# A macaron block of eight batches on one core: 384- and 128-column score blocks in one bank

## The chip, the core and the metric

The kernel runs as one program on one core of a Trainium2 chip. The metric is device time in microseconds from launch to end. The engines that matter are TensorE (PE in the profile: matmuls, with its weight loads as PEld), VectorE (DVE), ScalarE (ACT), GpSimd (POOL) and SyncE (SP), which issues the transfers. Each engine runs its own list of instructions in order, and the lists meet only at semaphores.

## The reference, cut to what matters

The input is 8 batches of 1024 tokens with 256 features. It passes through six residual layers: a gated feed-forward layer, a chunked linear attention, the feed-forward layer again, a routed low-rank layer, a softmax attention with rotary positions, and the routed layer once more. The change touches the softmax attention alone, which has 16 heads of 16 features:

```python
scores = jnp.einsum('bhqd,bhkd->bhqk', q, k) * scale
causal = jnp.triu(jnp.ones((S, S), dtype=bool), k=1)
scores = jnp.where(causal, -jnp.inf, scores)
attn = jax.nn.softmax(scores, axis=-1)
out = jnp.einsum('bhqk,bhkd->bhqd', attn, v)
```

## The kernel before, in words

Work on a batch has three parts. The **front** computes the first four layers and the rotary q, k and v for two halves of 512 tokens. The **core** is the softmax attention. The **tail** projects its result and runs the last routed layer. Core work on batch b lies beside front work on later batches and tail work on earlier ones.

The order of work is written out by `weave` (line 468), which every engine calls with its own pieces. Time is cut into ticks, 120 to a batch. In a tick an engine does a core step, if the tick has one (`CORE_TICKS`, line 387: four ticks of five), then a piece of each live front and tail. A core step is split into three parts, with front pieces of the two halves between them (parts 0, 1 and 2). On VectorE the core step comes one tick later than on the others (`lag` 1, line 1121). So a core step's place among front pieces is fixed ahead, and what an engine waits for there depends on how far the others have come.

The core works on groups of four heads, four groups to a batch, 32 in all. Each group has two passes over its scores.

The **first pass** finds each row's maximum. `score` (line 743) puts one bank of scores into one of two banks taken in turn by `r_take` (line 449), which waits until VectorE has emptied the bank two uses back. VectorE reduces it at lines 1104 and 1107. A group has 36 such banks, and this pass runs `LEAD` core steps ahead of the second. The maxima go through a transpose and a transfer by SP into two rows of `stq`, so that the second pass subtracts them by its matmul. The transposes of the maxima and of the results (`y_tr_at`) use the same two banks.

The **second pass** has transposed blocks: 128 keys down the partitions, up to 512 queries along the columns. A unit (`tunits`, line 366) is one half c of the queries, one block kb of keys and one pair hp of heads. Blocks below the diagonal have 512 columns. The four blocks that meet the diagonal have 512, 384, 256 and 128. A group has 24 units and each is one core step:

- `tscore(u + 1)` (line 754): for each head j of the pair one matmul into bank j, which waits until ScalarE has read unit u out of that bank.
- ScalarE's exponential (line 1310): two instructions, bank j to `pexp`.
- GpSimd's select (line 1458): zeroes what lies above the diagonal in a unit's first 128 columns, both heads in one instruction, for diagonal units only.
- `values(u - 1)` (line 769), in every second step: for both units of a key block four matmuls with 32 active columns each, one per head, added up in bank 2. At the end of a half ScalarE copies that bank to `ypv` (line 1316).

A step whose number u is even (u from 0 at the first step of the second pass) has `tscore`, one bank of `score`, the front's piece and `values`. An odd one has `tscore`, one bank of `score`, the front's piece and a second bank of `score` (line 396).

## Time and profile before

| | us |
|---|---|
| median of three runs | 2968.49 |
| the three runs | 2968.49, 2950.70, 2970.06 |
| the profiled execution | 2963.63 |
| its span, first to last instruction | 2961.9 |
| PE busy | 2640.6 (89%) |
| DVE busy | 1862.2 (63%) |
| ACT busy | 1230.0 (42%) |
| POOL busy | 754.6 (25%) |
| mean granted TensorE clock | 0.93 of 2.4 GHz |

Busy time is the time that an engine's rows cover. PE rows overlap and their ends are modelled, so a PE that is shown busy may be waiting for a part of it. The profiled execution lies 4.9 us under the median. Between 846 and 2576 us the trace repeats itself from batch to batch, every 348 us or a little less; from 2576 us on there is no front work left, and from 2907 us on no core work.

### The profile page before, as it was taken

How to read it: one execution, taken by the hardware profiler on the slowest of the kernel's cores; microseconds unless marked ns; L12 is line 12 of the kernel's file. 1: busy time of each engine (PE TensorE's matmuls, PEld its weight loads, DVE VectorE, ACT ScalarE, POOL GpSimd, SP SyncE). 2: the span in 40 equal slices, each digit the busy share in tenths (PEclk: the TensorE clock that was granted, in tenths of full speed). 3: DMA queues.
4: the chain of work that ended last, by engine and by line, in shares of the span. 5: the costliest groups of instructions: out<-in, count | busy, mean ns of one | idle time of the engine just before them, and what ended most of it. 6: DMA issues, size and time to landing. Idle time of an engine off the chain costs nothing.

```text
span 2961.9 us, 45503 instructions
## 1 busy us (share of the span) xinstructions
PE 2640.6 (89%) x15278; PEld 1740.0 (59%) x15278; DVE 1862.2 (63%) x5534; ACT 1230.0 (42%) x2802; POOL 754.6 (25%) x1283
## 2 busy tenths in 40 slices
PE   4885899899999999899999999989998999998986
PEld 3563666456655666466665666556664666555644
DVE  5544667666677567666667666675676666766642
ACT  1321244444444444444444444444444444444452
POOL 2321232223222232223322232222322233211111
PEclk8996899989999999999999899999999999999998
DMA  2015103411333113411134113331134121443211
GB/s 59 1 46 134 23 17 80 115 41 25 70 91 98 39 41 82 129 49 45 38 96 123 40 27 68 93 95 45 35 78 123 52 52 23 100 119 76 64 38 47
DMA packets 137423, 193.97 MB, mean 65 GB/s; under 512 B 49439, under 2 KB 111214, under 8 KB 127854
## 3 DMA queue, kind: packets, MB, share of 16 engines
q1 hardware_dynamic: 131808, 190.89, 25.9%
q8 instruction: 129, 2.11, 0.3%
q10 hardware_dynamic: 5390, 0.18, 0.1%
q14 instruction: 96, 0.79, 0.1%
HBM read 122.34 MB, written 67.63 MB: 64 GB/s over the span
## 4 chain that ended last, share of the span: by engine, by line
PE 71%; DVE 16%; DMA 4%; issue 3%; ACT 3%; POOL 2%; SPq 1%; DVEq 0%; ACTq 0%; POOLq 0%
PE bank L765 9%; PE bank L784 9%; PE bank L750 8%; PE bank L587 5%; PE bank L678 4%; PE bank L518 4%; PE bank L567 4%; PE bank L527 3%; PE bank L536 3%; PE bank L692 3%; DVE bank L1104 3%; PE bank L622 2%; PE bank L497 2%; PE bank L633 2%; PE bank L561 2%
## 5 line engine op out<-in xcount | busy, mean ns | idle before, releaser
L1310 ACT ACTIVATE pexp<-bank 128x512 f32<-128x512 f32 (+3 forms) x1536 | 675.8, 497 | 555.1 <-PE bank L765 554.9
L1104 DVE CUSTOM_DVE_ANT_0 bank<-bank,maskneg 128x256 f32<-128x256 f32 (+3 forms) x1024 | 484.9, 511 | 294.1 <-PE bank L750 291.5
L765 PE MATMUL bank<-stq,stk 128*128 128x512 f32 (+3 forms) x1536 | 558.6, 435 | 58.0 <-ACT pexp L1310 54.9
L750 PE MATMUL bank<-stk,stq 128*128 128x512 f32 (+3 forms) x1536 | 512.8, 399 | 100.1 <-DMA stk<-k_halves 31.3
L765 PEld LDWEIGHTS bank<-stq,stk 128*128 128x128 f32 x1536 | 274.5, 200 | 344.3 <-ACT pexp L1310 210.4
L1107 DVE TENSOR_REDUCE mxa<-bank 128x1 f32<-128x512 f32 x512 | 348.7, 685 | 133.2 <-PE bank L750 128.4
L1458 POOL TENSOR_SCALAR_AFFINE_SELECT pexp<-pexp 128x256 f32<-128x256 f32 x512 | 214.3, 425 | 743.0 <-ACT pexp L1310 742.6
L750 PEld LDWEIGHTS bank<-stk,stq 128*128 128x128 f32 x1536 | 288.2, 203 | 184.5 <-issue 120.6
L784 PE MATMUL bank<-pexp,vsm 128*32 128x512 f32 (+3 forms) x3072 | 360.9, 544 | 5.7 <-POOL pexp L1458 5.5
L1376 POOL TENSOR_SCALAR_AFFINE_SELECT arena<-arena 128x512 f32<-128x512 f32 x128 | 78.5, 638 | 416.3 <-ACT arena L1212 416.3
L587 PE MATMUL bank<-arena 32*128 32x256 f32 x1024 | 158.0, 428 | 17.2 <-DVE arena L911 14.2
L1327 POOL TENSOR_SCALAR varep<-mv 128x4 f32<-128x4 f32 x96 | 22.6, 235 | 488.6 <-DVE mv L822 488.6
L1129 ACT COPY xnT<-bank 128x512 f32<-128x512 f32 x160 | 88.8, 602 | 140.3 <-PE bank L497 140.1
L518 PE MATMUL bank<-arena,wk 128*128 128x256 f32 x512 | 141.0, 425 | 6.5 <-DVE arena L852 6.4
L497 PE MATMUL bank<-ident,arena 128*128 128x128 f32 x768 | 119.4, 306 | 30.7 <-DVE arena L828 29.9
L587 PEld LDWEIGHTS bank<-arena 32*128 32x128 f32 x1024 | 95.2, 198 | 69.8 <-issue 51.7
L497 PEld LDWEIGHTS bank<-ident,arena 128*128 128x128 f32 x768 | 101.3, 159 | 54.5 <-DVE arena L828 34.7
L1432 POOL TENSOR_TENSOR arena<-arena 128x1024 f32<-128x1024 f32 x32 | 75.8, 2368 | 224.1 <-DVE arena L1026 224.1
L784 PEld LDWEIGHTS bank<-pexp,vsm 128*32 128x32 f32 x3072 | 63.5, 112 | 117.5 <-issue 89.8
L911 DVE TENSOR_TENSOR arena<-bank,mask 128x512 f32<-128x512 f32 x128 | 82.2, 683 | 77.0 <-PE bank L587 77.0
L518 PEld LDWEIGHTS bank<-arena,wk 128*128 128x128 f32 x512 | 108.3, 217 | 37.5 <-DVE arena L852 10.8
L1150 ACT ACTIVATE arena<-bank 128x512 f32<-128x512 f32 x64 | 38.3, 598 | 207.0 <-PE bank L518 207.0
(186 smaller groups left out, 4204.3 us busy)
## 6 DMA issues: line engine op xcount, KB each, us to landing
stq<-q_halves SPq DMA_DIRECT2D x128, 256.0 KB
arena<-rope_table SPq DMA_DIRECT2D x8, 2048.0 KB
q_halves<-arena SPq DMA_DIRECT2D x32, 512.0 KB, 3.0
k_halves<-arena SPq DMA_DIRECT2D x32, 512.0 KB, 2.8
stk<-k_halves SPq DMA_DIRECT2D x64, 256.0 KB
stk<-k_halves SPq DMA_DIRECT2D x128, 128.0 KB
v_rows<-arena SPq DMA_DIRECT2D x16, 544.0 KB, 4.1
vsm<-v_rows SPq DMA_DIRECT2D x16, 544.0 KB, 3.8
```

What stands on the lines that cost most here:

```text
L497: last = nc.tensor.transpose(bk[:, t * P:(t + 1) * P], src[:, t, k * P:(k + 1) * P], ident[:])
L518: last = mm(bk[:, m * D:(m + 1) * D], wk0[:, k, m * P:(m + 1) * P], xmA[:, h, k], start=k == 0, stop=k == KT - 1)
L567: last = mm(bk, xn[:, k, j * P:(j + 1) * P], wqkv[:, k, D:3 * D], start=k == 0, stop=k == KT - 1)
L587: last = mm(bks[i][:, k * D:(k + 1) * D], khT[rows, k, j * P:(j + 1) * P], qbd[rows, j % 2, k], start=k == 0, stop=k == KT - 1, skip_group ...
L678: mm(bk[:, i * D:(i + 1) * D], xn[:, k, t * P:(t + 1) * P], wf1[:, k], start=k == 0, stop=False)
L750: last = mm(bk[:, col:col + n], stq[b_][:, h % 2, qb * P:(qb + 1) * P], stk[b_][:, h % 2, k0:k0 + n], start=True, stop=True)
L765: mm(ps(j)[:, 0:n], stk[b_][:, j, kb * P:(kb + 1) * P], stq[b_][:, j, (c + 1) * CH - n:(c + 1) * CH], start=True, stop=True).then_inc(s["t ...
L784: last = mm(ps(2)[HP * j:HP * (j + 1), CH - n:CH], vsm[:, kb, at:at + HP], pexp[:, (u - 1 + j // 2) % NPX, j % 2, 0:n], start=kb == 0, sto ...
L1104: last = nc.vector.tensor_tensor_reduce(out=sc, in0=sc, in1=maskneg[:, CH - n:CH], scale=1.0, scalar=LOWEST, op0=ALU.add, op1=ALU.max, acc ...
L1107: last = nc.vector.reduce_max(dst, sc, AX)
L1310: nc.scalar.activation(pexp[:, u % NPX, j, 0:n], ps(j)[:, 0:n], ACT.Exp, scale=DK ** -0.5).then_inc(s["exp_done"], 1)
L1458: nc.gpsimd.affine_select(out=v, in_=v, compare_op=ALU.is_ge, fill=0.0, base=0, pattern=[[0, 2], [1, P]], channel_multiplier=-1).then_inc( ...
```

## The change

Of the four diagonal blocks, those with 384 and 128 columns become one unit of two blocks, side by side in the same bank: blocks 4c+1 and 4c+3 of half c. A group has 20 units in place of 24, so a batch has 80 core steps in place of 96, on two ticks of three in place of four of five. `tscore` issues two matmuls per head for such a unit and signals after the second. One exponential of 512 columns reads both blocks. GpSimd issues one select for each block of a diagonal unit, as many as before. `values` issues eight matmuls for the merged unit, where there were two groups of four. No matmul is taken away or added. The number of ticks to a batch, the front and the tail stay as they were. The 36 banks of the first pass are spread over 20 steps in place of 24, and the constants that place loads, transposes and copies are rewritten for the new numbering, so that each falls on about the same tick.

```diff
-        tunits = [(c, kb, hp) for c in range(NC) for kb in range(4 * (c + 1)) for hp in range(2)]
+        tblocks = [(c, ((kb, CH, 0),)) for c in range(NC) for kb in range(4 * c + 1)]
+        for c in (1, 0):
+            at = [v[0] for v in tblocks].index(c) + 4 * c + 1
+            tblocks[at:at] = [(c, ((4 * c + 1, 3 * P, 0), (4 * c + 3, P, 3 * P))), (c, ((4 * c + 2, 2 * P, 0),))]
+        tunits = [(c, blocks, hp) for c, blocks in tblocks for hp in range(2)]
...
-        LEAD = 30
+        LEAD = 25
...
-        SX = 129
+        SX = 107
...
-            if (4 * tick) // 5 != (4 * (tick - 1)) // 5:
-                CORE_TICKS[tick] = (4 * tick) // 5
+            if (2 * tick) // 3 != (2 * (tick - 1)) // 3:
+                CORE_TICKS[tick] = (2 * tick) // 3
...
-            score_at[SX - LEAD + n // 3 * 2 + (n % 3 + 1) // 2, n % 3 // 2] = divmod(n, NSU)
+            step = n * NTU // NSU
+            score_at[SX - LEAD + step, 1 if n and (n - 1) * NTU // NSU == step else 0] = divmod(n, NSU)
...
-                        mm(ps(j)[:, 0:n], stk[b_][:, j, kb * P:(kb + 1) * P],
-                                  stq[b_][:, j, (c + 1) * CH - n:(c + 1) * CH], start=True, stop=True).then_inc(
-                                      s["t_ps"], 1)
+                        for kb, n, col in blocks:
+                            last = mm(ps(j)[:, col:col + n], stk[b_][:, j, kb * P:(kb + 1) * P],
+                                      stq[b_][:, j, (c + 1) * CH - n:(c + 1) * CH], start=True, stop=True)
+                        last.then_inc(s["t_ps"], 1)
...
-                    for j in range(G):
-                        at = VP * (G * (g % NG) + j)
-                        last = mm(ps(2)[HP * j:HP * (j + 1), CH - n:CH], vsm[:, kb, at:at + HP], pexp[:, (u - 1 + j // 2) % NPX, j % 2, 0:n],
-                                  start=kb == 0, stop=kb == 4 * c + 3, tile_position=(0, HP * j))
+                    for kb, n, col in blocks:
+                        for j in range(G):
+                            at = VP * (G * (g % NG) + j)
+                            last = mm(ps(2)[HP * j:HP * (j + 1), CH - n:CH], vsm[:, kb, at:at + HP],
+                                      pexp[:, (u - 1 + j // 2) % NPX, j % 2, col:col + n], start=kb == 0, stop=kb == 4 * c + 2,
+                                      tile_position=(0, HP * j))
...
-                        v = pexp[:, u % NPX, :, 0:P]
-                        nc.gpsimd.affine_select(out=v, in_=v, compare_op=ALU.is_ge, fill=0.0, base=0, pattern=[[0, 2], [1, P]],
-                                                channel_multiplier=-1).then_inc(s["causal"], 1)
+                        for _, _, col in tunits[u % NTU][1]:
+                            v = pexp[:, u % NPX, :, col:col + P]
+                            last = nc.gpsimd.affine_select(out=v, in_=v, compare_op=ALU.is_ge, fill=0.0, base=0, pattern=[[0, 2], [1, P]],
+                                                           channel_multiplier=-1)
+                        last.then_inc(s["causal"], 1)
```

**ScalarE, the last group of the last batch.** Before, the exponentials of both halves:

```order
L1310 ACTIVATE pexp<-bank 128x512 x4
L1310 ACTIVATE pexp<-bank 128x384 x2
L1316 COPY ypv<-bank 128x512
L1310 ACTIVATE pexp<-bank 128x384 x2
L1310 ACTIVATE pexp<-bank 128x256 x4
L1310 ACTIVATE pexp<-bank 128x128 x4
L1310 ACTIVATE pexp<-bank 128x512 x6
L1316 COPY ypv<-bank 128x512
L1310 ACTIVATE pexp<-bank 128x512 x14
L1310 ACTIVATE pexp<-bank 128x384 x4
L1310 ACTIVATE pexp<-bank 128x256 x4
L1310 ACTIVATE pexp<-bank 128x128 x4
```

The same group after the change (line numbers are those of the changed kernel; the first copy is that of the group before, in both):

```order
L1318 ACTIVATE pexp<-bank 128x512 x6
L1324 COPY ypv<-bank 128x512
L1318 ACTIVATE pexp<-bank 128x512 x2
L1318 ACTIVATE pexp<-bank 128x256 x4
L1318 ACTIVATE pexp<-bank 128x512 x6
L1324 COPY ypv<-bank 128x512
L1318 ACTIVATE pexp<-bank 128x512 x18
L1318 ACTIVATE pexp<-bank 128x256 x4
```

The eight instructions of 384 and the eight of 128 columns have become eight of 512: 40 exponentials in place of 48.

**TensorE, a stretch without front work in the second half of a group.** L765 is `tscore`, L750 `score`, L784 `values`. Before:

```order
L765 MATMUL bank<-stq,stk 128x512 x2
L750 MATMUL bank<-stk,stq 128x512
L784 MATMUL bank<-pexp,vsm 32x512 x4
L765 MATMUL bank<-stq,stk 128x384 x2
L750 MATMUL bank<-stk,stq 128x512 x2
L765 MATMUL bank<-stq,stk 128x384 x2
L750 MATMUL bank<-stk,stq 128x128
L750 MATMUL bank<-stk,stq 128x384
L784 MATMUL bank<-pexp,vsm 32x512 x4
```

After (`tscore` is L772, `score` L757, `values` L792):

```order
L772 MATMUL bank<-stq,stk 128x384
L772 MATMUL bank<-stq,stk 128x128
L757 MATMUL bank<-stk,stq 128x128
L757 MATMUL bank<-stk,stq 128x384
L757 MATMUL bank<-stk,stq 128x512
L772 MATMUL bank<-stq,stk 128x384
L772 MATMUL bank<-stq,stk 128x128
L772 MATMUL bank<-stq,stk 128x384
L772 MATMUL bank<-stq,stk 128x128
L757 MATMUL bank<-stk,stq 128x256 x2
L792 MATMUL bank<-pexp,vsm 32x512 x4
L757 MATMUL bank<-stk,stq 128x512
```

The merged step has four `tscore` matmuls, and the step with `values` now has a second bank of `score` behind it, here the row of 512 columns at the end, where before it had one bank.

## Rows read from the trace of the kernel before

**Rows 1.** Page, first part: busy time, share of the span, instructions

```profile
PE 2640.6 (89%) x15278; PEld 1740.0 (59%) x15278; DVE 1862.2 (63%) x5534; ACT 1230.0 (42%) x2802; POOL 754.6 (25%) x1283
```

**Rows 2.** Windows: stretch, length; busy (instructions) per engine; clock, DMA share, GB/s

```profile
1533.00:1881.00 348.00, 325.62 (x1905) 215.28 (x1904) 228.62 (x688) 152.92 (x350) 92.21 (x157) 0.94 0.28 68
```

**Rows 3.** Windows of line 765 alone: length; PE, PEld busy (instructions); clock, DMA

```profile
1533.00:1596.00 63.00, 18.76 (x50) 9.05 (x50) 0.95 0.42 115
```

**Rows 4.** PE's waits over the whole run: us in total, times, longest

```profile
PE bank L765 <- ACT pexp L1310: 54.9, 68, 2.2
PE bank L750 <- DVE mxa L1104: 29.9, 30, 2.3
PE bank L750 <- DVE mxa L1107: 25.7, 29, 2.8
PE bank L750 <- DVE mxb L1104: 11.2, 29, 1.2
PE bank L784 <- POOL pexp L1458: 5.5, 8, 0.7
PE bank L765 <- DMA stq<-mlo: 2.3, 1, 2.3
```

**Rows 5.** Timeline of PE, last group, no `score`: start, length, what

```profile
2881.22 0.48 PE L765 MATMUL bank<-stq,stk 128*128 128x128 f32 x2
...
2883.01 0.73 PE L765 MATMUL bank<-stq,stk 128*128 128x512 f32 x2
...
2885.52 0.96 PE L765 MATMUL bank<-stq,stk 128*128 128x512 f32 x2
...
2895.14 0.73 PE L765 MATMUL bank<-stq,stk 128*128 128x512 f32 x2
2896.38 0.99 PE L765 MATMUL bank<-stq,stk 128*128 128x512 f32 x2 [0.51 <-ACT pexp L1310]
...
2898.30 0.62 PE L765 MATMUL bank<-stq,stk 128*128 128x384 f32 x2
...
2901.14 0.50 PE L765 MATMUL bank<-stq,stk 128*128 128x256 f32 x2
...
2903.43 0.44 PE L765 MATMUL bank<-stq,stk 128*128 128x128 f32 x2
```

**Rows 6.** Timeline of PE, a stretch with `score` and without front work

```profile
1587.53 0.73 PE L765 MATMUL bank<-stq,stk 128*128 128x512 f32 x2
1588.10 0.74 PE L750 MATMUL bank<-stk,stq 128*128 128x512 f32 x3
1588.78 0.99 PE L765 MATMUL bank<-stq,stk 128*128 128x512 f32 x2
...
1590.93 0.73 PE L765 MATMUL bank<-stq,stk 128*128 128x512 f32 x2
```

**Rows 7.** Chain of waits, 2700 to 2740 us: start, length, what

```profile
2705.12 0.29 PE bank L750 x2
...
2711.15 0.24 PE bank L750
2711.39 0.99 PE bank L784 x8
...
2721.87 0.78 PE bank L784 x8
...
2727.96 0.36 PE bank L784 x8
```

**Rows 8.** Timeline of ACT, last group: two exponentials of 512, two of 128

```profile
2893.83 1.08 ACT L1310 ACTIVATE pexp<-bank 128x512 f32<-128x512 f32 x2 [0.17 <-PE bank L765]
...
2903.85 0.45 ACT L1310 ACTIVATE pexp<-bank 128x128 f32<-128x128 f32 x2 [0.66 <-PE bank L765]
```

**Rows 9.** Page, groups: busy and mean ns of one, then idle before

```profile
L1107 DVE TENSOR_REDUCE mxa<-bank 128x1 f32<-128x512 f32 x512 | 348.7, 685 | 133.2 <-PE bank L750 128.4
L1458 POOL TENSOR_SCALAR_AFFINE_SELECT pexp<-pexp 128x256 f32<-128x256 f32 x512 | 214.3, 425 | 743.0 <-ACT pexp L1310 742.6
```

More of the change, by code:

```diff
@@ L364, in macaron @@
         f_free = [s[f"f_free{i}"] for i in range(3)]
-        tunits = [(c, kb, hp) for c in range(NC) for kb in range(4 * (c + 1)) for hp in range(2)]
+        tblocks = [(c, ((kb, CH, 0),)) for c in range(NC) for kb in range(4 * c + 1)]
[3 more added lines that the diff above has]
+        tunits = [(c, blocks, hp) for c, blocks in tblocks for hp in range(2)]
         NTU = len(tunits)
+        N0 = sum(c == 0 for c, _, _ in tunits)
+        NLATE = sum(c == 1 and blocks[0][0] >= 4 for c, blocks, _ in tunits)
         packs = (((0, 0), (2, 0)), ((3, 0),), ((1, 0), (5, CH)), ((4, 0),), ((4, CH), (6, CH)), ((5, 0),), ((6, 0),), ((7, 0),),
@@ L380, in macaron @@
         NU = NTU * NG
-        DIAG = [u for u, (c, kb, hp) in enumerate(tunits) if kb >= 4 * c]
-        LEAD = 30
+        DIAG = [u for u, (c, blocks, hp) in enumerate(tunits) if blocks[0][0] >= 4 * c]
+        LEAD = 25
         FT = 120
         F_AT = [(FT * b + 4, FT * b + 26) for b in range(NB)]
-        SX = 129
+        SX = 107
         S_END = SX + NU * NB + 8
         CORE_TICKS = {}
-        for tick in range(S_END * 5 // 4 + 2):
-            if (4 * tick) // 5 != (4 * (tick - 1)) // 5:
-                CORE_TICKS[tick] = (4 * tick) // 5
+        for tick in range(S_END * 3 // 2 + 2):
+            if (2 * tick) // 3 != (2 * (tick - 1)) // 3:
+                CORE_TICKS[tick] = (2 * tick) // 3
         G_AT = [FT * (b + 3) for b in range(NB - 2)] + [1014, 1134]
@@ L399, in macaron, with width @@
         for g in range(NG * NB):
-            y_tr_at[SX + NTU * g + 11] = (g, 0)
+            y_tr_at[SX + NTU * g + N0 + 3] = (g, 0)
             y_tr_at[SX + NTU * (g + 1) + 3] = (g, 1)
-        sums_at = {SX + NTU * g + (10, NTU + 2)[c]: (g, c) for g in range(NG * NB) for c in range(NC)}
-        def width(c, kb):
-            return CH - max(0, kb - 4 * c) * P
+        sums_at = {SX + NTU * g + (N0, NTU)[c] + 2: (g, c) for g in range(NG * NB) for c in range(NC)}
+        def width(blocks):
+            return sum(n for _, n, _ in blocks)
         def slot(g, hp):
@@ L756, in tscore @@
                     g, i = divmod(u, NTU)
-                    c, kb, hp = tunits[i]
+                    c, blocks, hp = tunits[i]
                     if i == 0:
                         nc.tensor.wait_ge(max_in[g % 2], 64 * (g // 2 + 1))
-                    n = width(c, kb)
                     b_ = slot(g, hp)
@@ L1303, in core_act @@
                         g, i = divmod(u, NTU)
-                        c, kb, hp = tunits[i]
-                        n = width(c, kb)
+                        n = width(tunits[i][1])
                         if u >= NPX:
@@ L1513, in core_sp @@
                     for b in range(NB):
-                        for k, at in enumerate((SX + NU * b - 7, SX + NU * b + 3)):
+                        for k, at in enumerate((SX + NU * b - NLATE + 1, SX + NU * b + 3)):
                             if t == at:
```

8 lines of the change are left out of this document (4 added, 4 removed).

## The prediction, made before the change had run

> **What bounds the kernel now.** Start with the busy times. PE is busy 89% of the span, DVE 63%, ACT 42%, POOL 25% [rows 1]. In one period of the steady part PE is busy 325.6 of 348 us and DVE 228.6 [rows 2]. So an engine that is not PE can set the time only where PE waits for it. The list of PE's waits says how often that is: 54.9 us in 68 waits for the exponentials, 29.9 + 25.7 + 11.2 = 66.8 us in 88 waits of `score` for VectorE's reductions, 5.5 us for GpSimd's selects [rows 4]. These are waits that the profile sees; a shorter one lies hidden in the modelled ends of the matmuls.
>
> Then ask how PE is paced where it has no front work. In the last group there is no `score` either. A pair of steps with 512 columns takes 2898.30 - 2895.14 = 3.16 us, and its first half, without `values`, takes 2896.38 - 2895.14 = 1.24 us, of which PE idles half a microsecond for ScalarE [rows 5]. With `score` beside it and the same lack of front work, the half without `values` takes 1588.78 - 1587.53 = 1.25 us although three more matmuls (two banks) run in it: they are hidden in the wait. The other half takes 1590.93 - 1588.78 = 2.15 us, against 3.16 - 1.24 = 1.92 without its one bank: there a bank costs 0.23 us [rows 6]. So thin stretches go by the exponentials' round trip, and the rest by PE's own work.
>
> How much is thin? One stretch of 63 us has 50 of the period's 192 `tscore` rows, that is 25 of 96 steps at 2.5 us each, where the mean is 348/96 = 3.6 us [rows 3]. With the shorter thin pieces elsewhere I take a third of the steps; a quarter and a half are the ends.
>
> **The change, part by part.** The sum is made against the profiled execution, 2963.6 us, which lies 4.9 us under the median of the runs, 2968.5.
>
> *PE's stream.* Matmuls and columns are the same before and after. Nothing is saved on them by themselves.
>
> *Fewer calls of `values`.* A call of 512, 384 and 128 columns takes 0.99, 0.78 and 0.36 us on the chain [rows 7]: 0.21 us for each 128 columns and 0.15 us per call. Merging turns 0.78 + 0.36 into 0.99 and saves 0.15 us. There are 2 merged key blocks in each of 32 groups: 64 x 0.15 = 9.6 us. This is PE's own time, so it counts in thick stretches too.
>
> *Fewer round trips, in thin stretches.* The pairs of steps from one start of `tscore` to the next take 2.84 us (384), 2.29 (256), 1.79 (128) and 2.51 (the 512 that follows, which has the 128's `values` in it) [rows 5]: together 9.43. After the change they are 3.16 (merged), 2.29 + 0.21 and 2.51 + 0.21, since `values` trails by a pair and each now has 128 columns more: 8.38. So 1.05 us per merge, 2.1 per group, the 0.15 of each call within it.
> Against it stands `score`. A group's 36 banks now go on 20 steps. The ten without `values` have room for two each, and take 18; the ten with `values` get 18 where 12 had 12. Six more banks at 0.23 us are 1.4 us. Net: 0.7 us per group that is thin. The core work after the front's end, from 2576 to 2907 us, is about six groups: at 24 steps of 1.7 us [rows 6] 331 us would hold eight, and the tail's work lies between. Of the 26 groups beside front work a third is 9, and of the five that follow I take the whole: 14 x 0.7 = 10 us. The last group has no `score` and keeps its 2.1 us.
>
> *Thick stretches.* The other 17 groups keep 2 x 0.15 = 0.3 us each, 5 us in all. Every step is also a point at which PE waits for ScalarE to have caught up; 16 fewer in 96 are a sixth of 54.9, or 9 us.
>
> *ScalarE.* Two exponentials take 1.08 us at 512 columns and 0.45 at 128 [rows 8]: 0.21 per 128 columns and 0.24 fixed. 128 merged units save 0.24 us each, 31 us of ScalarE. It is covered by PE, which is twice as busy; where the cover is gone, it is already in the round trips above. I count nothing more.
>
> *GpSimd.* The selects are as many as before, but the merged unit's two follow each other, and `values` waits for the second: 0.425 us more [rows 9]. `values` comes a whole exponential pair (1.08 us) after its unit's, so this hides. Uncovered in all 128 units it would be 54 us; the 5.5 us of waits [rows 4] say that the cover holds. Zero, with 5 as the upper end.
>
> *SyncE and the transfers.* Loads, row transfers and copies keep their ticks within half a tick. The one that gets tighter is the transfer of the maxima: it has 3 steps in place of 4 before the second pass needs it. It waited once, 2.3 us, in the last group [rows 4]. A step of thin work is about 1.7 us [rows 6], so up to 1.7 us in each of the last five groups: 0 to 8 us, I take 2. No queue is moved past another's work.
>
> *VectorE's two banks.* This is the unknown. A bank of `score` waits for the reduction of the one two back. Before, steps of one and of two banks take turns, four of them on successive ticks and then a tick without. After, two steps on successive ticks have two banks each (one step in five has one), and then comes a tick without. A bank in the second of the two waits for a reduction of 0.685 us [rows 9] that VectorE begins one tick late, with the front's work ahead of it. The tick without a step lets VectorE catch up. The trace cannot show the new pattern. Its waits now cost 66.8 us; a third less is -22 and two thirds more +45. I take +10, near the present cost, since the number of banks is the same and the wait falls partly on time in which PE would have waited for ScalarE.
>
> *The sum.* -10 (thin) -2 (last group) -5 (calls) -9 (sync points) +2 (maxima) +10 (banks) = -14 us. 2963.6 - 14 = 2949.6; I forecast **2950**.
>
> *A rule against it.* One bank of two matmuls stands at 0.29 us in the chain and one of a single matmul at 0.24 [rows 7], so a merged bank reaches ScalarE 0.05 us later than one of 512 columns. The Trainium skill (Perfetto Trace Analysis, "Matmuls") wants independent matmul groups to rotate through banks, so that the evacuation of one overlaps the next, and says in the same place that larger matmuls are more efficient; by the first the merge gives overlap away, by the second it gains. At 0.05 us for 256 banks the loss is 13 us at most, a third of that where the pace is thin: 4 us, inside the range.
>
> **The rivals.**
> *The gain is larger (2915).* PE's busy rows hide waits, so the round trip rules more than a third of the steps. For it: half a microsecond of waiting in a step that shows 0.73 us busy of 1.24 [rows 5]. If all 31 groups with neighbours gain 1.05 x 2 - 1.4 = 0.7 us, if waits for ScalarE and VectorE (121.7 us) fall by a sixth, 20 us, and the banks cost nothing: 22 + 2 + 20 = 44 us, so 2920; some 5 us come on top if the granted clock (0.94 in the period, rows 2) gains from fewer gaps: one hundredth of it is worth 348 x 0.01/0.94 = 3.7 us a period at most. The Trainium skill (Perfetto Trace Analysis, "Identifying the Most-Contended Engine") holds that matmul occupancy is a poor measure of TensorE's headroom and that weight-load occupancy is better; that row is 59% here [rows 1], which agrees with hidden waits. Against it: thick stretches have front matmuls in nearly every step.
> *Slower (3001): the two banks.* In 320 of 640 steps, the second of each two, both banks wait for reductions that VectorE starts in that same tick. Waits of this kind last 66.8/88 = 0.76 us on average and up to 2.8 [rows 4]. At 0.075 us more per such step the 24 us of savings are gone; from 0.18 on the time is over 2998; one full wait in every fourth step, 0.19 us, gives 2963.6 - 24 + 61 = 3001. For it: VectorE is two thirds busy and in order, and its core work comes a tick late. Against it: no reductions lie on the tick before the first of the two steps.
> *Nothing moves (2964).* Instructions on PE are as before and its order is fixed by ticks that have not moved; a wait taken out reappears at the next front piece, which waits for VectorE or ScalarE at the same tick.
>
> **How the numbers follow.** Runs of this kernel spread over 19 us, so within 1% (2939 to 2998 about the median) counts as no change. Forecast, net -14 us, own range 2930 to 2968: 0.45, of which 0.13 under 2939. Larger gain: 0.22. Nothing moves: 0.13. Slower: 0.20, of which 0.17 over 2998. Faster 0.13 + 0.22 = 0.35; slower 0.17; the same 0.48. The range goes from 2905, the larger gain with a better clock, to 3005.
>
> **What would show it.** Exponentials 1280, ACT busy about 1200 us; calls of `values` 320; in the last group a merged pair at 3.16 us and 20 steps where 24 were; PE's waits for the exponentials under 50 us. Right if `score`'s waits for VectorE are 60 to 90 us. Wrong if they pass 110 us (the slower rival) or fall under 50 (the larger gain), or if `values` waits for GpSimd over 10 us.

## The result: slower by 21 us, and the profile after

The changed kernel takes 2985.39 us (median of 12 runs, 2969.74 to 3006.44) against 2964.16 for the kernel before (12 runs, 2950.70 to 2970.06). The ratio is 1.0079, 95% interval 1.0056 to 1.0101: slower, by less than 1%. The forecast was 2950, 14 us faster than the profiled execution of the kernel before; the time moved the other way. The profiled execution took 2974.95 us (span 2973.2), 10 us under its median, so its trace shows about half of the loss.

The page's busy times and two steady periods of the changed kernel (windows: length; busy time and instructions of PE, PEld, DVE, ACT, POOL; granted clock, DMA share, GB/s):

```profile
PE 2601.8 (88%) x15278; PEld 1741.7 (59%) x15278; DVE 1874.9 (63%) x5534; ACT 1194.4 (40%) x2546; POOL 749.6 (25%) x1283
```

```profile
1599.00:1947.00 348.00, 317.78 (x1912) 212.99 (x1904) 229.81 (x688) 148.13 (x319) 91.89 (x156) 0.96 0.27 69
1947.00:2295.00 348.00, 317.67 (x1912) 213.25 (x1904) 229.80 (x688) 148.09 (x319) 91.84 (x156) 0.96 0.27 68
```

ACT fell by 36 us, where 31 had been worked out. PE is busy 318 us of a period, against 326 in [rows 2], and the period is 348 us in both. That looks as if PE had saved 8 us, but the two stretches have different clocks, 0.96 and 0.94. The kernel before also has a period at 0.96 (columns as above):

```profile
1191.00:1532.00 341.00, 318.31 (x1906) 210.99 (x1904) 228.08 (x688) 152.74 (x350) 92.12 (x157) 0.96 0.28 70
```

At the same clock PE is busy for the same time, and the changed kernel's period is 7 us longer: 7 us more in which PE stands. PE's waits over the whole run say where (us in total, times, longest; line 757 is `score`, 772 `tscore`, 792 `values`, 594 the scores of the linear attention):

```profile
PE bank L772 <- ACT pexp L1318: 70.0, 71, 2.2
PE bank L757 <- DVE mxa L1113: 33.9, 39, 2.5
...
PE bank L757 <- DVE mxb L1113: 28.5, 27, 1.7
PE bank L757 <- DVE mxa L1116: 23.1, 47, 2.8
...
PE bank L594 <- DVE arena L920: 21.6, 20, 3.1
...
PE bank L757 <- DVE mlo L1090: 5.6, 7, 1.0
...
PE bank L772 <- DMA stq<-mlo: 4.2, 4, 2.0
...
PE bank L792 <- POOL pexp L1467: 3.5, 6, 0.6
```

The waits for exponentials rose from 54.9 to 70.0 us, where I had expected under 50. `score`'s waits for reductions rose from 66.8 to 33.9 + 28.5 + 23.1 = 85.5 [rows 4]; with the 5.6 for the row maxima they are the 91 of the expectations below. Of the waits that the sum had priced, only those for the selects fell, from 5.5 to 3.5.

The last group, with no `score` and no front, went as forecast. PE's timeline there (start, length, what, in brackets the idle time before it):

```profile
2908.84 0.79 PE L772 MATMUL bank<-stq,stk 128*128 128x384 f32 x4
2910.09 0.99 PE L772 MATMUL bank<-stq,stk 128*128 128x384 f32 x4 [0.46 <-ACT pexp L1318]
...
2912.00 0.51 PE L772 MATMUL bank<-stq,stk 128*128 128x256 f32 x2
```

The merged pair takes 2912.00 - 2908.84 = 3.16 us, the figure put down for it. From the last addition that GpSimd does for a front to the end, the kernel before needs 2961.9 - 2625.7 = 336.2 us and the changed one 2973.2 - 2643.5 = 329.7, 6.5 less (sum: 5.6). The first row is of the kernel before, the second of the changed one:

```profile
2625.71 2.37 POOL L1432 TENSOR_TENSOR arena<-arena 128x1024 f32<-128x1024 f32 x1 [8.54 <-DVE arena L1026]
```

```profile
2643.53 2.36 POOL L1440 TENSOR_TENSOR arena<-arena 128x1024 f32<-128x1024 f32 x1 [7.28 <-DVE arena L1035]
```

So where the core runs by itself, merging shows a gain of the size that was worked out, in one profile each. The loss, 18 us by 2643, lies where front and core share the engines. By the last such addition of each batch the changed kernel is behind by 2.7 us at 898 us, 10.9 at 1251 and 18.2 at 1599; after that nothing is added, since the kernel before takes 348 us for its later periods too, at clocks of 0.94 and 0.95.

### The profile page after: what moved, and what is told of

It is laid out like the page before. It is cut to its first block, busy times and chain, and to the rows that moved or that the text cites. A ratio compares the mean times of both kernels' runs of the same rounds, so it can differ in the third digit from the quotient of the medians.

```text
span 2973.2 us, 45061 instructions
## 1 busy us (share of the span) xinstructions
PE 2601.8 (88%) x15278; PEld 1741.7 (59%) x15278; DVE 1874.9 (63%) x5534; ACT 1194.4 (40%) x2546; POOL 749.6 (25%) x1283
## 4 chain that ended last, share of the span: by engine, by line
PE 65%; DVE 15%; issue 3%; DMA 3%; ACT 2%; POOL 2%; SPq 1%; POOLq 0%; DVEq 0%; ACTq 0%
PE bank L757 9%; PE bank L792 8%; PE bank L772 8%; PE bank L594 4%; PE bank L685 4%; PE bank L525 3%; PE bank L534 3%; PE bank L574 3%; PE bank L543 3%; PE bank L504 3%; PE bank L699 2%; DVE mxa L1116 2%; DVE bank L1113 2%; DVE arena L837 2%; DMA arena<-x_rows 2%
## 5 line engine op out<-in xcount | busy, mean ns | idle before, releaser
L1318 ACT ACTIVATE pexp<-bank 128x512 f32<-128x512 f32 (+1 forms) x1280 | 644.9, 562 | 374.6 <-PE bank L772 374.5
L757 PE MATMUL bank<-stk,stq 128*128 128x512 f32 (+3 forms) x1536 | 549.1, 407 | 122.7 <-DVE mxa L1113 33.9
L772 PE MATMUL bank<-stq,stk 128*128 128x512 f32 (+3 forms) x1536 | 499.9, 411 | 74.6 <-ACT pexp L1318 70.0
L757 PEld LDWEIGHTS bank<-stk,stq 128*128 128x128 f32 x1536 | 283.5, 198 | 374.1 <-issue 319.5
L772 PEld LDWEIGHTS bank<-stq,stk 128*128 128x128 f32 x1536 | 280.1, 201 | 227.8 <-ACT pexp L1318 161.8
L792 PE MATMUL bank<-pexp,vsm 128*32 128x512 f32 (+3 forms) x3072 | 341.1, 534 | 7.1 <-POOL pexp L1467 3.5
L594 PE MATMUL bank<-arena 32*128 32x256 f32 x1024 | 148.6, 407 | 29.3 <-DVE arena L920 21.6
L504 PE MATMUL bank<-ident,arena 128*128 128x128 f32 x768 | 116.8, 302 | 34.1 <-DVE arena L837 33.1
L792 PEld LDWEIGHTS bank<-pexp,vsm 128*32 128x32 f32 x3072 | 70.3, 112 | 129.4 <-issue 106.7
L1221 ACT COPY arena<-bank 128x512 f32<-128x512 f32 x128 | 68.8, 589 | 163.2 <-PE bank L594 163.2
```

The source lines that it names most:

```text
L504: last = nc.tensor.transpose(bk[:, t * P:(t + 1) * P], src[:, t, k * P:(k + 1) * P], ident[:])
L594: last = mm(bks[i][:, k * D:(k + 1) * D], khT[rows, k, j * P:(j + 1) * P], qbd[rows, j % 2, k], start=k == 0, stop=k == KT - 1, skip_group ...
L757: last = mm(bk[:, col:col + n], stq[b_][:, h % 2, qb * P:(qb + 1) * P], stk[b_][:, h % 2, k0:k0 + n], start=True, stop=True)
L772: last = mm(ps(j)[:, col:col + n], stk[b_][:, j, kb * P:(kb + 1) * P], stq[b_][:, j, (c + 1) * CH - n:(c + 1) * CH], start=True, stop=True)
L792: last = mm(ps(2)[HP * j:HP * (j + 1), CH - n:CH], vsm[:, kb, at:at + HP], pexp[:, (u - 1 + j // 2) % NPX, j % 2, col:col + n], start=kb = ...
L1318: nc.scalar.activation(pexp[:, u % NPX, j, 0:n], ps(j)[:, 0:n], ACT.Exp, scale=DK ** -0.5).then_inc(s["exp_done"], 1)
```

## The experiments

Times are medians, with the ratio to the kernel before on the same chip and its 95% interval.

**First question: the reductions, or the ticks without a step?** In the two light kernels VectorE reduces only the last 128 columns of each block, so a part of the maximum is left out.

```diff
-                            sc = r_bank("s", g, i)[:, col:col + n]
+                            sc = r_bank("s", g, i)[:, col + n - P:col + n]
```

> The changed kernel with VectorE's reduction of each first-pass score block cut to its last 128 columns (part of the maximum is left out), so that a bank of scores is handed back early. Two theories of the 21 us by which the change is slower (2985 against 2964). Theory 'banks': PE waits on VectorE for the banks of bunched scores (91 us in the changed kernel, 67 before). Then this kernel's waits of the score line on VectorE fall under 35 us and it comes out 5 to 20 us FASTER than the kernel before with the same cut (the next run), since the loss is gone and the fewer core steps remain. Theory 'empty ticks': PE waits longer on ScalarE's exponentials and on the front's chains because the core steps stand in two of three ticks. Then this one stays 12 us or more SLOWER than the kernel before with the same cut, and its waits on exponentials stay at 65 us or more.

> The kernel before with the same cut of VectorE's reduction to 128 columns of each block: the partner of the run above. By both theories its score waits on VectorE fall from 67 us to under 30 and the time falls by 15 to 50 us, to 2915 to 2950; what is compared is this time against the changed kernel's with the same cut: 5 to 20 us above it by 'banks', 12 us or more below it by 'empty ticks'.

Measured: 2913.50 (0.983, 0.9804 to 0.9857) for the changed kernel and 2864.52 (0.9662, 0.9637 to 0.9687) for the one before. The cut gains 72 us in the one and 96 in the other, where 15 to 50 had been expected of e2. `score`'s waits for reductions are 39 and 26 us. Cheaper reductions don't take the loss away: it grows from 21 to 49 us, as "empty ticks" had it, and e1's waits for exponentials are 76.5 us. The length of a reduction, on which my price for the banks rested [rows 9], isn't what the change costs by.

**Second: the placement of the banks alone.** e3 takes the changed kernel and places its 36 banks of a group by ticks, not by core steps; one function more, called by PE and by VectorE in each tick, carries it. e4 does the reverse to the kernel before: two banks in three of four steps.

```diff
-            step = n * NTU // NSU
-            score_at[SX - LEAD + step, 1 if n and (n - 1) * NTU // NSU == step else 0] = divmod(n, NSU)
+            tick = n * 30 // NSU
+            score_at[(SX - LEAD) * 3 // 2 + tick, 1 if n and (n - 1) * 30 // NSU == tick else 0] = divmod(n, NSU)
```

```diff
-            score_at[SX - LEAD + n // 3 * 2 + (n % 3 + 1) // 2, n % 3 // 2] = divmod(n, NSU)
+            score_at[SX - LEAD + n // 2 + n // 6, n % 2] = divmod(n, NSU)
```

> The changed kernel with its full reductions, but the first-pass scores no longer tied to core steps: 36 banks spread evenly over the 30 ticks of a group, ticks without a core step included (six banks in five ticks, against two in nearly every core step and none in every third tick). 'Banks': the score waits on VectorE fall from 91 us to 50 to 70, and the time to 2958 to 2972. 'Empty ticks': what is lost is the wait for exponentials and front chains in the pattern of ticks, which stays: 2978 to 2992; a bank in the tick without a core step gives PE a little work there, so up to 5 us may come back.

> The kernel before with one thing changed, the placement of the first-pass scores: two banks in three of four core steps and none in the fourth, in place of 2, 1 and 1 or so; no tick, unit or exponential moves. 'Banks': score waits on VectorE rise from 67 us to 85 to 100 and the time by 10 to 22 us, to 2974 to 2986. 'Empty ticks': the placement hardly matters: 2960 to 2970.

Measured: e3 2949.35 (0.9955, 0.9937 to 0.9974), e4 3000.55 (1.0130, 1.0103 to 1.0157). The placement alone turns the change from 21 us slower to 11 us faster, and it slows the unchanged units by 40. Neither theory had these two right: e3 is below both ranges and e4 above both. The granted clock doesn't explain the placement's worth. Among the runs with a clock of 0.935, the changed kernel took 2976.01 us, e3 2950.52, e8 (below) 2945.86 to 2950.13 in four, and the kernel before 2954.10 to 2964.02 in three. So about 26 of the 36 us are there at an equal clock; the rest goes with the lower clock of the changed kernel (median of its runs 0.930, of e3's 0.937), and what lowers it isn't shown. These are the waits of e3 (line 761 is `score`, 776 `tscore`):

```profile
PE bank L761 <- DVE mxb L1119: 53.1, 40, 2.2
PE bank L776 <- ACT pexp L1326: 48.1, 66, 2.2
PE bank L761 <- DVE mxa L1119: 46.0, 56, 2.0
...
PE bank L761 <- DVE mxa L1122: 15.7, 24, 2.8
```

The waits for exponentials fell to 48.1, as the forecast had them. `score`'s waits for reductions rose again, to 115 us, in the faster kernel. The list names what PE waits for last at each place; it isn't the price of that place.

**Third: is it cover, and what is the merging worth with banks placed alike?**

```diff
 e5: the placement of e3 with the cut of e1
 e6: the kernel before, with
+            tick = n * 30 // NSU
+            score_at[124 + tick, 1 if n and (n - 1) * 30 // NSU == tick else 0] = divmod(n, NSU)
 e7: the changed kernel, with
+        for step in range(S_END + 1):
+            CORE_TICKS[6 * (step // 4) + step % 4 + 2] = step
 e8: the placement by ticks, with
+        BANK_TICKS = sorted([*range(30), 1, 7, 10, 16, 22, 25])
```

> The changed kernel with the banks spread over all ticks (2949 with full reductions) and VectorE's reduction cut to 128 columns per block as in the two light runs (2914 for the changed kernel, 2865 for the one before). The spreading took 36 us off the changed kernel while PE's score waits on VectorE did not fall (91 before it, 115 and more after). Theory 'ring': the spreading acts on how soon VectorE hands a bank back; with the cut that hardly limits any more, so little is left to gain: 2900 to 2914. Theory 'cover': a bank of scores is PE's own work that stands between a chain's steps (exponential, front reductions); a tick without one leaves the chain bare, and a quicker VectorE doesn't mend that: the spreading gives 30 to 50 us here too, 2862 to 2884, about the kernel before with the same cut.

> The kernel before with the same spreading of the banks over all 30 ticks of a group (its own placement is three banks in two core steps, in four of five ticks, so nearly even). If the merging itself is worth what the sum gave it (about 15 to 20 us from steps, values calls and last groups), this stays near the kernel before, 2950 to 2966, and the merged kernel with the same spreading (2949) is the faster by that. If the merging is worth nothing, this comes to 2940 to 2952 as well.

> The changed kernel with four core steps in a row and then two ticks without, in place of two and one; banks stay tied to steps. 'Cover': two ticks in a row without banks and steps are barer still: 2995 to 3030. 'Ring': second banks of four steps follow one another, so slower as well, 2990 to 3010, with score waits on VectorE over 100 us; what tells them apart is where PE waits: 'cover' has it on exponentials and front lines, their sum up by 20 us or more.

> The changed kernel with one bank in every tick and the six second banks of a group put into ticks without a core step (in the even spreading most of them fall beside a core step). 'Cover': the ticks without a step are the barest, so a little more comes back: 2935 to 2948. 'Ring': two banks in one short tick wait for VectorE: 2950 to 2965.

Measured: e5 2860.78 (0.966, 0.9636 to 0.9684), e6 2980.20 (1.0058, 1.0036 to 1.0080), e7 3017.56 (1.0186, 1.0163 to 1.0210), e8 2947.22 (0.9955, 0.9940 to 0.9969). With the cut, the placement is worth 53 us (2913.50 to 2860.78), more than the 36 without: again not the reductions' length. "Cover" had e7 and e8 in its ranges and missed e5 by 1 us; "ring" had e5, e7 and e8 wrong. In e7 PE waits at the front's lines, whose chains have no core work beside them for two ticks (lines 503 and 524 stand where 504 and 525 do in the changed kernel, which had 33.1 and 8.2 us):

```profile
PE bank L771 <- ACT pexp L1317: 76.6, 66, 3.6
PE bank L503 <- DVE arena L836: 55.1, 21, 6.8
...
PE bank L524 <- DVE arena L860: 25.5, 8, 3.4
```

`score`'s waits for reductions in e8, as fast as e3, are larger still, 138 us:

```profile
PE bank L762 <- DVE mxb L1120: 55.2, 50, 1.9
...
PE bank L762 <- DVE mxa L1120: 46.5, 44, 2.0
PE bank L762 <- DVE mxa L1123: 36.2, 54, 2.8
```

e6 is slower than the kernel before, and above both of its ranges: even spacing isn't good in itself.

**Fourth: a rule for the doubles?** Banks per kind of tick, in the order tick with a step and no `values`, tick without a step, tick with step and `values`: 1, 2, 0.6 (e9), 2, 1, 0.6 (e10), 1, 0.6, 2 (e11), against 1, 1.6, 1 in e8 and 1.8, 0, 1.8 in the changed kernel. e12 is the kernel before with its doubles in ticks without a step.

```diff
 e9
+        BANK_TICKS = sorted([t for t in range(30) if t % 3 < 2] + [t for t in range(30) if t % 3 == 1] + [2, 8, 11, 17, 23, 26])
 e10
+        BANK_TICKS = sorted([t for t in range(30) if t % 3 < 2] + [t for t in range(30) if t % 3 == 0] + [2, 8, 11, 17, 23, 26])
 e11
+        BANK_TICKS = sorted([t for t in range(30) if t % 3 != 1] + [t for t in range(30) if t % 3 == 2] + [1, 7, 10, 16, 22, 25])
 e12
+        BANK_TICKS = sorted([*range(30), 2, 7, 12, 17, 22, 27])
```

> The changed kernel, banks per kind of tick (a tick with a core step but no values call, an empty tick, a tick with a step and a values call): 1, 2, 0.6 in place of the changed kernel's 1.8, 0, 1.8 and the 1, 1.6, 1 of the run before. The steps with a values call last 3.8 us in the changed kernel and the two ticks without one together 5.0, 3.6 and 5.0 where second banks lie in empty ticks. Theory 'even ticks' (PE's own work of a tick must be even, since the chains of the other engines move on one tick at a time): better again, 2930 to 2945. Theory 'ring' (banks must come evenly, whatever lies between): two banks in every empty tick are bunched, 2952 to 2970.

> Banks per kind of tick 2, 1, 0.6: the doubles stand beside the core steps that have no values call. 'Even ticks': the values ticks are as light as in the run before this one, the rest is nearly even: 2932 to 2950. 'Ring': 2952 to 2970, as any two in a tick. If what the second bank harms is the exponential of the same step, by standing between the score block and the values, it is slower than the doubles in empty ticks by 10 us or more.

> The opposite: banks per kind of tick 1, 0.6, 2, the doubles in the ticks that have the values call as well. 'Even ticks': most of the loss is back, 2970 to 2990, though banks are no more bunched than in the two runs before. 'Ring': the same as those two, 2952 to 2970.

> The kernel before with one bank in each tick and the six second ones in its empty ticks (one in five): the placement that gave 2947 with the merged blocks. It tells what the merging is worth with banks placed alike: at 2955 to 2970 the merging is worth 8 to 20 us, as the sum without its term for the banks has it; at 2940 to 2950 the merging is worth nothing and the placement all. 'Even ticks' expects it below the spreading that put all doubles beside values calls (2980), by 10 us or more.

Measured: e9 2959.88 (0.9979, 0.9961 to 0.9997), e10 3000.58 (1.0110, 1.0083 to 1.0136), e11 3002.45 (1.0113, 1.0088 to 1.0138), e12 3025.70 (1.0204, 1.0177 to 1.0231). "Even ticks" falls with e10, and "ring" with the 41 us between e9 and e10, which are bunched alike. e12 is the worst, with the placement that was the best for merged units. "Cover" falls as an account of the time as well: e10 and e12 have a bank in every tick without a step, and are among the slowest. It does describe the waits for exponentials in the merged kernels, 36.7 to 48.6 us with a bank or more in such a tick (e3, e8, e9, e10), 70.0 and 72.5 with none or 0.6 (the changed kernel, e11). So e10's loss, though of the size that was put down for a second bank that harms the exponential, isn't that: its waits for exponentials are 40.3 us, below e8's 48.6. None of the rules put down for kinds of ticks holds.

What goes with the time in most of these kernels is VectorE's idle time just before its two reduction lines, that is, the time in which it stands at a reduction until PE has written the bank (sum of the two groups, one profile each):

| kernel | VectorE idle before reductions, us | median, us |
|---|---|---|
| before | 427.3 | 2964 |
| e8, e14 | 444.4, 453.3 | 2947, 2957 |
| e9, e3 | 453.7, 457.2 | 2960, 2949 |
| e6 | 461.8 | 2980 |
| e10, e12 | 484.4, 490.1 | 3001, 3026 |
| e13, changed | 490.2, 492.3 | 2981, 2985 |
| e11, e4 | 500.2, 500.4 | 3002, 3001 |

This is a sign and not a price. The kernel before has the least and isn't the fastest, and e12 is 25 us slower than e10 with 6 us more. e7, where the core's ticks moved as well, has 446.5 at 3018 and doesn't fit. The light kernels, whose reductions are shorter, have 573 (e2), 622 (e5) and 686 (e1) at 2865, 2861 and 2914. The groups in the changed kernel and in e8 (busy and mean ns of one, then idle time before them):

```profile
L1113 DVE CUSTOM_DVE_ANT_0 bank<-bank,maskneg 128x256 f32<-128x256 f32 (+3 forms) x1024 | 486.7, 510 | 323.6 <-PE bank L757 319.0
...
L1116 DVE TENSOR_REDUCE mxa<-bank 128x1 f32<-128x512 f32 x512 | 349.3, 688 | 168.7 <-PE bank L757 159.6
```

```profile
L1120 DVE CUSTOM_DVE_ANT_0 bank<-bank,maskneg 128x256 f32<-128x256 f32 (+3 forms) x1024 | 483.7, 510 | 243.8 <-PE bank L762 241.9
L1123 DVE TENSOR_REDUCE mxa<-bank 128x1 f32<-128x512 f32 x512 | 349.7, 686 | 200.6 <-PE bank L762 197.1
```

The trace of before showed this column too: 133.2 us of it stand in [rows 9]. I had read it as idle time of an engine that isn't the bottleneck. Since VectorE works in order, it is time in which the front's pieces behind the reduction stand still as well.

**Fifth: one bank, and VectorE's order alone.** A stall of the kind that the slower rival described is in the trace, in the 12th tick of a batch. PE and VectorE there:

```profile
1640.61 0.50 PE L757 MATMUL bank<-stk,stq 128*128 128x512 f32 x1
1640.95 0.69 PE L772 MATMUL bank<-stq,stk 128*128 128x384 f32 x4
1643.92 0.55 PE L757 MATMUL bank<-stk,stq 128*128 128x256 f32 x1 [2.27 <-DVE mxa L1113]
```

```profile
1638.59 1.40 DVE L861 SCALAR_TENSOR_TENSOR arena<-xnT,mu,arena 128x512 f32<-128x512 f32 x2
1639.91 1.37 DVE L837 TENSOR_SCALAR arena<-arena,mv,rstd 128x256 f32<-128x256 f32 x4
1641.20 1.39 DVE L828 BATCH_NORM_STATS2 stats<-arena 128x6 f32<-128x256 f32 x4
1642.63 0.38 DVE L831 BATCH_NORM_AGGREGATE mv<-stats 128x2 f32<-128x6 f32 x4
1642.92 0.27 DVE L1113 CUSTOM_DVE_ANT_0 bank<-bank,maskneg 128x128 f32<-128x128 f32 x1
```

VectorE isn't idle; it has 4.5 us of front pieces ahead of the reduction for which PE stands 2.27 us. The Trainium skill (PSUM — Partial Sum Buffer, "Engine vs sequencer instructions") says that VectorE's queue is strictly first in, first out. These rows agree: the reduction comes behind all the front pieces ahead of it.

e13 moves one of the 144 banks of a batch so that this stall goes; e14 brings it into e8. e15 and e16 leave PE's order alone and shift VectorE's reductions by half a tick; e17 and e18 shift them by less.

```diff
 e13: the changed kernel's placement, written by ticks, and
+            if tick % 120 == 11:
+                tick, part = tick - (part == 0), 0
 e14: e8, for the first group of each batch
+        ONE_MOVED = sorted([*range(30), 1, 8, 10, 16, 22, 25])
 e15: VectorE's two reductions of a tick, in the next tick, each behind one front piece
-                                core(at, 1 + q)
+                                core(at, q if lag else 1 + q)
 e16: e8, the two directly behind the front pieces of their own tick
+                            if first and lag and q < NC:
+                                first(tick, q)
 e17: the changed kernel, at the end of their own tick (e18: the same in e8)
+                            if at is not None and lag and q in (1, 3):
+                                core(at, (1, 3).index(q))
```

> The changed kernel with ONE bank of the 144 of a batch moved: of the two that stand in the 11th tick of each batch, the first goes into the empty 10th. In the changed kernel PE stands 2.3 us at the first bank of the 12th tick, since the two banks of the 11th lie unreduced behind 4.5 us of VectorE's front pieces (normalization and mixing of the next stage); the triple of ticks 12 to 14 takes 16.2 us there and 12.1 with doubles in empty ticks. Theory 'queue' (a bank is held until VectorE has passed the front pieces that stand ahead of its reduction, so it costs only beside such pieces): 3 to 4 us per batch, less what is recovered behind: 2958 to 2972. Theory 'even' (what counts is how evenly the banks of all ticks lie): one of 144 changes nothing, 2980 to 2990.

> The mirror: the version with doubles in empty ticks (2947) with one bank of each batch moved from the empty 10th tick to the 11th, so that two lie ahead of the 12th again. 'Queue': 2958 to 2975. 'Even': 2944 to 2950.

> The changed kernel with VectorE's reductions half a tick later in its own order (each behind one more of VectorE's front pieces); PE's order is as it was, no instruction is added. 'Queue': every bank is held behind one more piece: 3010 to 3080, with the score waits on VectorE well over 120 us. If the place in VectorE's queue doesn't matter: 2980 to 2990.

> The version with doubles in empty ticks (2947), with VectorE's reductions half a tick earlier (a tick's two reductions directly behind that tick's own front pieces). 'Queue': the banks come back earlier: 2925 to 2945, unless VectorE now stands at a reduction for PE and holds its front pieces up, 2950 to 2975; then VectorE's idle time ahead of the reductions rises over the 457 us or so of the changed kernel's.

> The changed kernel with PE's order untouched and VectorE's reductions only a little earlier: the first of a tick ahead of the tail's pieces of the same tick, the second at the end of its tick, ahead of the next tick's first front piece in place of behind it. 'Queue' (a bank costs by what stands ahead of its reduction): the second banks come back one front piece sooner, 2955 to 2978. If VectorE now stands at the reductions for PE as it did with all of them half a tick early (850 us idle ahead of them, 3100), 2990 to 3050. If the order of VectorE's queue isn't what the second banks cost by: 2980 to 2990.

> The same small shift of VectorE's reductions in the version with doubles in empty ticks (2947): second banks are 6 of 36 there, not 16 of 36, so 'queue' has little to give back, 2935 to 2950; if VectorE stands for PE, 2955 to 3000.

| | median, us | ratio, interval | VectorE idle before reductions, us |
|---|---|---|---|
| e13 | 2981.28 | 1.0076, 1.0049 to 1.0103 | 490.2 |
| e14 | 2956.67 | 0.9986, 0.9974 to 0.9998 | 453.3 |
| e15 | 3032.90 | 1.0247, 1.0226 to 1.0268 | 361.3 |
| e16 | 3099.93 | 1.0470, 1.0449 to 1.0490 | 850.0 |
| e17 | 3035.14 | 1.0238, 1.0221 to 1.0256 | 701.8 |
| e18 | 2979.30 | 1.0045, 1.0028 to 1.0062 | 593.9 |

e15 to e18 show that the place of a reduction in VectorE's order sets the time, both ways, with the same work on every engine. Half a tick later PE stands for banks (151 us of `score`'s waits, as expected) and 48 us are lost, although VectorE idles least of all there. Earlier, VectorE stands for PE: 32 us lost in e18, 50 in e17, 153 in e16. (The 457 us in the expectation of e16 are e3's idle time; the changed kernel has 492.3.) In e17 the banks did come back sooner: `score`'s waits for reductions fell from 85.5 to 65.3 us. What VectorE holds up by standing costs more. PE's waits for VectorE in the front, 33.1 + 21.6 + 8.2 = 62.9 us in the changed kernel, are 97.2 in e17:

```profile
PE bank L598 <- DVE arena L924: 41.1, 34, 5.5
PE bank L508 <- DVE arena L841: 37.9, 14, 6.8
...
PE bank L529 <- DVE arena L865: 18.2, 15, 3.4
```

In e18 neither sum moves much from e8's (138 and 52 us, against 138 and 47), so its 32 us don't show in the list. Of the four orders tried on the changed kernel and e8, the one that the program had is the best.

e13 and e14 tell what one such stall is worth. Bringing it in costs 9.5 us (the intervals of e8 and e14 don't overlap): over the seven batches with a front beside them 1.4 us each, where the stall is 2.3. Taking it out gains 4 us that can't be told from nothing. So e13 came where "even" had it and missed "queue", and e14 lies between the two. The stretch of 24 ticks from the stall on shows what comes back (windows of e13, then of the changed kernel, in the same batch: ticks 12 to 14; from there to the 33rd tick; ticks 33 to 35; tick 33 alone; columns as above):

```profile
1633.60:1647.00 13.40, 12.29 (x83) 10.10 (x79) 8.55 (x32) 6.55 (x14) 3.19 (x7) 1.00 0.00 0
1647.00:1706.90 59.90, 54.42 (x256) 34.46 (x253) 39.35 (x133) 25.12 (x61) 13.73 (x22) 0.91 0.17 40
1706.90:1722.40 15.50, 15.50 (x102) 11.74 (x99) 7.43 (x19) 5.53 (x11) 3.45 (x8) 0.78 0.14 37
1706.90:1714.60 7.70, 7.70 (x31) 6.06 (x28) 4.58 (x12) 1.07 (x2) 2.69 (x6) 0.57 0.28 74
```

```profile
1640.90:1657.10 16.20, 13.93 (x80) 11.13 (x79) 8.52 (x33) 6.31 (x13) 3.19 (x7) 0.89 0.01 1
1657.10:1714.00 56.90, 51.07 (x256) 32.30 (x253) 38.53 (x131) 25.00 (x61) 13.09 (x21) 0.98 0.17 43
1714.00:1727.10 13.10, 13.10 (x102) 9.97 (x99) 7.79 (x21) 5.53 (x11) 4.09 (x9) 0.96 0.16 44
1714.00:1719.40 5.40, 5.40 (x32) 4.36 (x29) 4.94 (x14) 1.07 (x2) 2.59 (x6) 0.89 0.39 106
```

Without the stall the first stretch is 2.8 us shorter. Then the same 256 and 102 PE instructions take 75.4 us in place of 70.0, at clocks of 0.91 and 0.78 in place of 0.98 and 0.96. In this batch the saved wait came back, and more, as time at the lower clock. It is the batch with the longest stretch of e13: its 24 ticks take 88.8 us here and 86.5, 83.5, 87.4 and 86.5 in the four others with a full front, against 86.2 to 86.3 in four of the changed kernel's and 91.5 in the fifth. So the return differs from batch to batch. In e14 the three ticks take 16.5 us where e8 has 12.1, in four of the five batches, and there nothing of it comes back within the 24 ticks (88.0 to 88.3 us, against 83.5 to 83.9).

## Why the prediction was wrong

The step that failed is "VectorE's two banks", +10 us: the sum took the new placement of the banks for nearly free, and it costs more than all the other terms gain.

- *Its size.* With the merged units kept and the banks placed otherwise the time is 2949 and 2947, so the placement costs 36 to 38 us (about 26 at an equal clock). The range of that step, -22 to +45, held it; the value I took was the present cost of the waits, not the new pattern's.
- *Its mechanism.* I priced a wait of PE for a reduction of 0.685 us. The cut of the reductions leaves the loss (49 us), and `score`'s waits for reductions are larger in the faster placements (115 us in e3, 55.2 + 46.5 + 36.2 = 138 in e8) than in the changed kernel (85.5). The shifts of VectorE's order show what the sum left out. Two queues, each worked in order, hand each other banks. PE may stand for a bank whose reduction lies behind VectorE's front pieces (e15); VectorE may stand for a bank that PE has not yet written, and then holds up the front pieces that PE needs next (e16, e17). My sum saw the first half alone. The 65.0 us that VectorE stands longer in the trace after (492.3 - 427.3, 59 of it named as waits for `score`) fit the second half. That this half makes the loss of the changed kernel is argued and not shown: no run takes it away by itself.
- *The test I set.* 85.5 us of waits count as "right" (60 to 90) where the time was wrong, and e3 has the 115 of "wrong" and is faster than the kernel before. The test was a poor one.

The other terms:

- *Fewer round trips and calls, -10, -2 and -5: right where they can be seen.* The merged pair takes 3.16 us. The stretch behind the last front is 6.5 us shorter (sum: 5.6, or 3.6 with the maxima's 2). But e13, which differs from the changed kernel by one bank in each batch, needs 336.4 us there, at a clock of 0.89 where the changed kernel has 0.91, so the 6.5 isn't clear of the clock. What the terms are worth beside front work was not measured by itself. Waits for GpSimd fell to 3.5 us, and the maxima's transfer cost 1.9 us more (sum: 2).
- *The front's end.* It is not at 2576 us: the front's last matmuls run to 2624 us and its last addition starts at 2625.7. That leaves 5.6 groups behind it (268 rows of `tscore`, 48 to a group) where I took six, a difference of under half a microsecond in the sum.
- *Sync points, -9: right only where a bank lies between.* The waits for exponentials fell by 6.8 us in e3 and to 48.6 in e8, but rose by 15 us in the changed kernel, whose ticks without a step have no bank either.
- *The rule set against it.* The prediction let larger matmuls speak for the change; but the merge makes no matmul larger, only the exponentials, so nothing was to be had there.
- *Together.* Without the term for the banks the sum was -24. The best placements measured are 11 to 13 us under the kernel before, which would make these terms about half right in front of the whole kernel. But a period of e8 takes 341.2 to 341.7 us in four of five, at clocks of 0.95 to 0.97, and one of the kernel before 341.3 at 0.96, while e8 is 4 to 18 us faster among the whole runs at 0.935. So a part of the 11 to 13 us may come with the clock, and how much isn't shown. With one placement for both, merging is worth 31 us (e6 to e3) or 78 (e12 to e8); how much of that is the merging and how much a placement that suits one of them isn't settled.

Of the rivals, "slower, the two banks" had the sign, its place (the second of two steps) and a wait that the trace shows in the 12th tick, but not the price of it: filling that wait gave nothing that can be measured. Its threshold was a little off too: 0.18 us in 320 steps gives 2997, not over 2998. "The gain is larger" wanted the waits for ScalarE and VectorE to fall by a sixth, and both rose. "A wait taken out reappears" held in some batches of e13, in the one shown through the clock rather than the next front piece.

What stays open: which pairs of ticks make the 36 us. By the mean start times of the ticks over four batches, the largest loss to e8 is 4.1 us in ticks 12 to 14 for the changed kernel, 3.5 in ticks 54 to 56 for e10, and 3.8 in ticks 21 to 23 for e11; e10 loses 2.8 in ticks 21 to 23 too, and e11 3.6 in ticks 12 to 14. These are few places, and the largest is another one each time. No rule that I tried foretold e10 or e12.

The version with doubles in ticks without a step (e8, 2947.22 us, 0.9955, 0.9940 to 0.9969) is, with e3, the fastest with whole reductions: 13 us under the kernel before on its chip, and 38 under the changed kernel.

## What to carry to other kernels

When fewer steps must carry the same side work, the side work is spaced anew as well: measure the steps and the placement apart. Placing it by time helped here in e3, e8 and e9, and did not in e6, e10, e11 and e12, so try several placements. Where two engines hand buffers to each other in fixed orders, look at the idle time of both ahead of the handover, and at what stands behind each; the idle time of an engine that isn't the bottleneck is free only if nothing that the bottleneck needs lies behind it. A sum of waits for one resource is no price: `score`'s waits for reductions rose by 52 us from the changed kernel to e8 while the time fell by 38.

## What was not expected of the hardware

Runs of the changed kernel spread over 37 us, and their times follow the mean granted clock: 3006.44 us at 0.922, 2982.51 at 0.930, 2969.74 at 0.938. The two levels are 1.2 and 2.4 GHz. In the rows above, tick 33 took 7.7 us at 0.57, near the lower level, in e13 and 5.4 us at 0.89, near the upper one, in the changed kernel, with PE busy throughout in both. The Trainium skill (TensorE: Matmul & The Clock Gate, "HAM oscillation — how this bites in real kernels") tells that long idle gaps in PE's work bring the lower clock, and shows it on waits for transfers. No run here tests that: in the batch shown, the kernel with a gap of 2.27 us filled had the lower clock behind it. Why it was granted there isn't shown: PE's busy share in the windows ahead is alike, 54.42 of 59.90 us and 51.07 of 56.90. Whole periods show it too. With the same 1905 instructions of PE in the same order, the five periods of the kernel before take 344.8, 341.3, 348.2, 348.3 and 348.0 us, at 0.95, 0.96, 0.94, 0.94 and 0.95; the changed kernel takes 348 at 0.96. Two periods of equal length can thus hide 7 us of waits, so compare the clocks first.
